# All loads on one queue in order of need, a batch's stack in two halves, maxima in groups of four heads

## The chip, the cores and the metric

The kernel runs on 1 core of one Trainium2 chip. The metric is the device time of one execution in microseconds. The time before is the median of 3 runs.

## What is computed

The reference is a chain of four layers on x of shape 2 x 256 x 128, with a context of 2 x 512 x 128. Layer by layer, cut to what matters here:

```python
x = x + xattn0(layernorm(x), ctx, ctx, mask, Wq, Wk, Wv, Wo, bo)   # 16 heads of 8, masked softmax
x = x + ffn0(layernorm(x), W_router, b_router, W1, b1, W2, b2)     # 8 experts, top 2, 128 -> 512 -> 128
x = x + xattn1(layernorm(x), ctx, cos, sin, ..., Wq, Wkv, Wo, bo)  # 16 heads of 64, ctx normed, rope on k, clip
x = x + ffn1(layernorm(x), weight, bias)                           # ternary weights, inputs rounded to 8 bit
```

In the first attention `scores = q @ k.T / sqrt(8)`, masked, and softmax over the 512 context tokens. Everything is float32. The second attention works on a layer-normed context; its k and v come from `ctx @ Wkv`.

## The kernel before

One program, five engines, each with an instruction stream of its own; the streams meet at semaphores. The order of the work in the middle is a list `order`, written out by hand, which TensorE, VectorE, ScalarE and GpSimd all walk, each doing its part of every item. SyncE only issues DMAs.

**Start.** SyncE loads x, l0w (four 128 x 128 weights), the transposed context `ctxT` in two halves and the context by tokens `ctx_tok` (L317). ScalarE's queue loads the mask twice, lncol, wv1 (the second attention's value weights), rows of ones, and then eight small arrays (L476). VectorE norms x to y (L598 to L609), with GpSimd's power -0.5 in between (L403). TensorE makes k of batch 0, transposes y, makes k of batch 1, q and v. ScalarE copies y transposed (L500), q (L502) and v (L506).

**Stacks.** The scores of the first attention are computed in bfloat16, with k and q each split in three bfloat16 parts, so that their products add up to float32's precision. VectorE splits batch 0 (L633 to L644), GpSimd batch 1 (L426 to L434). For a head, the 8 rows of every part have to stand under each other: `Ks` and `Qs` hold 72 rows of parts, 3 of the mask and 3 of the maxima for each of 16 heads. This layout is made through DRAM: SyncE stores the k parts (L333, three stores of 128 KB, 1 KB rows) to `k_scr` and the q parts (L340, 512 B rows) to `q_scr`, and reads them back into 24 partitions at a time: three reads of 384 KB for k (L343, 16 KB rows) and three of 192 KB for q (L347, 8 KB rows). A whole batch's stack is 1.73 MB. SyncE does batch 0 and then batch 1, in order: stores, mask rows, q store, k reads, q reads. All of it is in one queue.

**Maxima.** Softmax needs the maximum of each row of scores. An item `("mx", q, i)` is a matmul of 128 queries against 512 tokens for one head and VectorE's reduction of it to `nmax` (L661); there are 64, in 4 groups of 16 (8 heads, 2 query tiles). After a group `("mt", q)` transposes its maxima (L916), VectorE and GpSimd split them in three (L670, L671, L444, L445), and SyncE writes them as three rows of `Qs` (L355, 4 KB each), which the scores `("st", u)` of these heads wait for.

**Order of the middle.** Four values (`values(n)`, a matmul of 128 x 512 for the second attention's v) come ahead of it (`EARLY`). Then each of the other twelve values follows two maxima, and two more maxima come. Then 32 units u (batch and head): scores in bfloat16 (four matmuls), one more maximum, the product with v of an earlier unit (`pv`, float32), one more maximum; ScalarE takes the exponential of each unit (L539). The output projection, norm and router of batch 0 are put between units 20 to 29. Then come 16 expert steps (`hid`, `yy`), the second attention, and the last layer. The weights w1, w2, wk1, cosT and sinT are loaded on ScalarE's queue at units 1, 6, 12 and 16 to 19 (L476).

**The context's norm.** VectorE takes the statistics of `ctx_tok` after the q parts (L598), GpSimd the power, VectorE the shift (L650), ScalarE applies them (L511), TensorE transposes, ScalarE writes `ctxT` (L517), and the values follow.

The waits that matter here, in TensorE's part:

```python
if u % 8 == 0:
    pe.wait_ge(max_rows[u // 8], 16 * NPART)
...
if q % 2 == 0 and i == 0:
    ...
    pe.wait_ge(stack[b], 16 * 2 * NPART)
```

## Time and profile before

| what | us |
|---|---|
| median of 3 runs | 285.23 |
| lowest, highest | 282.26, 286.27 |
| the profiled execution | 283.63 |
| its span | 281.9 |
| mean granted TensorE clock | 0.954 of 2.4 GHz |

The span is the time from the first to the last instruction of the profiled execution; its whole time is 1.7 us longer. Shares of the span that the engines are busy: PE 87%, VectorE (DVE) 62%, ScalarE (ACT) 42%, GpSimd (POOL) 16%. PE is TensorE's matmuls, PEld its weight loads, SPq and ACTq are DMA issues on SyncE's and ScalarE's queue. A busy PE is not a PE at its peak: its matmuls overlap, and their ends are modelled. L661 is line 661 of the kernel. A window's columns are: its bounds and length, each engine's busy us with the number of instructions, the granted clock as a fraction, the mean busy share of the 16 DMA engines, and GB/s.

### The profile page before, as it was taken

Reading aid. Unit: us, or ns where it says so; the run is one execution under the profiler, and the core shown is the slowest. Engines: PE = TensorE matmul, PEld = TensorE weight load, DVE = VectorE, ACT = ScalarE, POOL = GpSimd, SP = SyncE. Lnnn points to the kernel's source line nnn. Section 1 sums busy time; section 2 is a strip of 40 time slices with the busy share of each in tenths; the row PEclk is TensorE's granted clock in tenths of the full one; section 3 lists DMA queues with packets and bytes.
Section 4 is the critical chain, followed back from the end, with each engine's and each line's share of the span. In section 5 each row is a group of like instructions: output and inputs, shape, how many; then the busy total and the mean of one; then the engine's idle time right before and its main releaser. Section 6 shows DMA issues by size and latency. Waiting matters only on the chain.

```text
span 281.9 us, 5069 instructions
## 1 busy us (share of the span) xinstructions
PE 244.6 (87%) x2004; PEld 157.2 (56%) x2004; DVE 175.4 (62%) x383; ACT 117.0 (42%) x180; POOL 45.1 (16%) x65
## 2 busy tenths in 40 slices
PE   0632979999999989999999999999979999999941
PEld 0232333343344548888897787886646668666630
DVE  0761049998884341556566962087986975899543
ACT  0226324376667965342424234546336350625000
POOL 2419100000000100051333633001200000100010
PEclk9995579999999999999999999999999999999985
DMA  4958446148721200006005063500000000000001
GB/s 137 239 140 118 113 137 138 45 154 279 203 73 48 76 2 0 2 0 149 3 21 131 0 149 74 136 16 3 0 2 2 0 2 2 0 2 3 2 1 38
DMA packets 13501, 18.63 MB, mean 66 GB/s; under 512 B 2188, under 2 KB 8196, under 8 KB 13188
## 3 DMA queue, kind: packets, MB, share of 16 engines
q1 hardware_dynamic: 9230, 11.95, 18.1%
q10 hardware_dynamic: 4246, 6.34, 7.5%
q8 instruction: 16, 0.26, 0.4%
q14 instruction: 9, 0.07, 0.1%
HBM read 12.45 MB, written 1.45 MB: 49 GB/s over the span
## 4 chain that ended last, share of the span: by engine, by line
PE 63%; issue 13%; DMA 10%; DVE 9%; ACT 2%; POOL 1%; SPq 1%; POOLq 0%; DVEq 0%; ACTq 0%
PE b L848 38%; PE st L848 22%; DVE nmax L661 6%; DMA reg_q<-q_scr 5%; DMA x<-in_x 2%; DMA m_scr<-mpart 2%; DMA q_scr<-reg_z 2%; PE b L947 1%; ACT reg_p L580 1%; ACT reg_p L539 1%; POOL rstd L403 1%; PE b L852 1%; SPq L347 0%; DVE st L598 0%; DVE y L609 0%
## 5 line engine op out<-in xcount | busy, mean ns | idle before, releaser
L661 DVE TENSOR_REDUCE nmax<-b 128x1 f32<-128x512 f32 x64 | 41.3, 685 | 21.0 <-PE b L848 20.9
L848 PE MATMUL b<-reg_p,v 128*32 128x256 f32 (+1 forms) x768 | 50.3, 382 | 1.1 <-ACT reg_z L545 1.1
L580 ACT ACTIVATE reg_p<-st 128x1024 f32<-128x1024 f32 x32 | 31.0, 1022 | 44.4 <-PE st L848 44.4
L557 ACT ACTIVATE reg_z<-st,b 128x256 f32<-128x256 f32 x56 | 24.5, 473 | 32.8 <-PE st L848 32.8
L539 ACT ACTIVATE reg_p<-st 128x1024 f32<-128x1024 f32 x32 | 31.9, 1022 | 9.6 <-PE st L848 6.7
L848 PEld LDWEIGHTS b<-w,reg_z 128*128 128x128 f32 x256 | 30.9, 192 | 4.9 <-issue 4.5
L848 PE MATMUL st<-v,reg_k 64*128 64x256 f32 x256 | 32.0, 389 | 0.3 <-ACT reg_p L580 0.2
L848 PEld LDWEIGHTS b<-reg_p,v 128*32 128x32 f32 (+1 forms) x768 | 19.9, 103 | 22.0 <-issue 9.8
L848 PE MATMUL b<-w,reg_z 128*128 128x128 f32 x256 | 31.5, 276 | 0.0
L794 DVE TENSOR_SCALAR reg_p<-reg_p 128x1024 f32<-128x1024 f32 x32 | 22.5, 703 | 11.3 <-ACT reg_p L580 11.3
L403 POOL TENSOR_TENSOR rstd<-ve,mhalf 128x2 f32<-128x2 f32 (+2 forms) x10 | 8.7, 871 | 123.0 <-DVE ve L603 123.0
L848 PEld LDWEIGHTS st<-v,reg_k 64*128 64x128 f32 x256 | 23.7, 186 | 7.9 <-issue 3.8
L848 PE MATMUL b<-reg_k,reg_q 75*128 75x512 bf16 x64 | 23.6, 396 | 4.1 <-DMA reg_q<-q_scr 2.3
L848 PE MATMUL st<-yT,w 128*128 128x256 f32 x112 | 26.8, 382 | 0.0
L848 PEld LDWEIGHTS st<-yT,w 128*128 128x128 f32 x112 | 20.2, 190 | 2.8 <-issue 0.4
L801 DVE TENSOR_TENSOR w<-reg_p 128x512 f32<-128x512 f32 x30 | 20.8, 692 | 1.0
L848 PE MATMUL st<-reg_p,ctxT 128*128 128x512 f32 x32 | 19.7, 722 | 1.0 <-ACT ctxT L517 1.0
L760 DVE SCALAR_TENSOR_TENSOR x<-b,wgt,x 128x128 f32<-128x128 f32 x32 | 9.6, 342 | 16.0 <-PE b L848 16.0
L848 PEld LDWEIGHTS b<-reg_k,reg_q 75*128 75x128 bf16 x64 | 6.2, 98 | 23.7 <-DVE nmax L661 20.3
L848 PE MATMUL st<-reg_q,reg_k 78*128 78x256 bf16 x128 | 19.2, 273 | 0.1
L496 ACT ACTIVATE v<-st 128x512 f32<-128x512 f32 x16 | 9.6, 597 | 18.7 <-PE st L848 18.7
L806 DVE RECIPROCAL rs<-b 128x256 f32<-128x256 f32 x8 | 14.0, 1752 | 3.7 <-PE b L848 3.7
(158 smaller groups left out, 264.5 us busy)
## 6 DMA issues: line engine op xcount, KB each, us to landing
reg_k<-k_scr SPq DMA_DIRECT2D x6, 384.0 KB
w<-in_w ACTq DMA_DIRECT2D x1, 2048.0 KB, 9.2
reg_k<-reg_p SPq DMA_DIRECT2D x16, 128.0 KB, 2.3
reg_k<-reg_q SPq DMA_DIRECT2D x16, 128.0 KB, 2.3
reg_q<-q_scr SPq DMA_DIRECT2D x6, 192.0 KB
k_scr<-reg_z SPq DMA_DIRECT2D x6, 128.0 KB
ctxT<-in_ctxT SPq DMA_DIRECT2D x2, 256.0 KB, 7.5
reg_p<-in_wv ACTq DMA_DIRECT2D x1, 512.0 KB, 8.5
```

The costliest lines, as they stand in the source:

```text
L403: nc.gpsimd.tensor_tensor(rstd[:, first:first + tiles], ve[:, first:first + tiles], mhalf[:, :].broadcast_to([P, tiles]), ALU.pow).then_in ...
L496: nc.scalar.activation(v1[:, n // 2, 512 * (n % 2):512 * (n % 2) + 512], bank[n % 4], ACT.Copy).then_inc(v1_sb, 1)
L539: nc.scalar.activation(prob[:, u % RING, :], st2[u % 2][:, :], ACT.Exp).then_inc(st_exp, 1)
L557: nc.scalar.activation(hT[:, n % 2, f, :], hidden(n, f), ACT.Relu, bias=b1[:, n % E, f:f + 1]).then_inc(h_sb, 1)
L580: nc.scalar.activation(prob[:, u % RING1, :], st2[u % 2][:, :], ACT.Exp, scale=DK1 ** -0.5).then_inc(st_exp, 1)
L661: nc.vector.tensor_reduce(nmax[:, q, i:i + 1], bank[4 + mx % 2], AX.X, ALU.max, negate=True).then_inc(mx_done, 1)
L760: last = nc.vector.scalar_tensor_tensor(out=x[:, b * QT + t, :], in0=bank[4 + n % 2][:, t * D:(t + 1) * D], scalar=wgt[:, b * QT + t, e:e ...
L794: nc.vector.tensor_scalar(prob[:, u % RING1, :], prob[:, u % RING1, :], math.exp(-CLIP), math.exp(CLIP), ALU.max, ALU.min).then_inc(clippe ...
L801: nc.vector.tensor_tensor(hsum[:, u % RING1, :], prob[:, u % RING1, 0:2 * S], prob[:, u % RING1, 2 * S:4 * S], ALU.add).then_inc(summed, 1)
L806: nc.vector.reciprocal(rs1[:, g % 2, :], bank[7][:, 0:S]).then_inc(rs_sb, 1)
L848: return nc.tensor.matmul(o, l, r, start=start, stop=stop)
L852: last = nc.tensor.transpose(dst[:, t * P:(t + 1) * P], src[:, first + t, :], ident[:, :])
```

## The change

- Every load at the start is issued on SyncE's queue: x, context by tokens, l0w, first half of the transposed context, the two masks, its second half, wv1, and the small arrays, seven of which are packed on the host in one array `small`, and b2. x, ctx, l0w, w1, w2 and wo1 are laid out on the host so that each partition's row is one piece. cosT and sinT are one array, loaded once.
- On VectorE the context's statistics stand before the norm's application to x and before k and q parts; the shift stands between k and q parts. ScalarE norms the context before it copies v, and signals each half. It also runs one exponential on a constant early (`warm`).
- TensorE makes q before k of batch 1.
- Batch 0's stack is read in two halves of eight heads (rows of 8 KB and 4 KB), each with a semaphore of its own. Batch 1's stack is read as before. Its four stores are issued on ScalarE's queue, the three of k ahead of ScalarE's copies of the values and the one of q after the second.
- Six values come ahead of the middle instead of four, ten after pairs of maxima, and no extra maxima before the first scores. Units 0 to 7 have three maxima each, later ones two.
- Maxima are grouped by four heads: 8 groups of 8, so 8 transposes, splits and 3-row writes, and scores wait for a group every 4 units. The rows are 2 KB each.
- w1, w2, wk1 and the rotation tables are loaded at units 6, 11, 16 and 18.

```diff
@@ -216,27 +218,26 @@
...
         order = []
-        maxima = [("mx", q, i) for q in range(2 * B) for i in range(H)]
+        maxima = [("mx", q, i) for q in range(QG) for i in range(4 * QT)]
...
                     order.append(("mt", order[-1][1] - 1))
-            if order[-1][0] == "st" and ("mt", 2 * B - 1) not in order:
-                order.append(("mt", 2 * B - 1))
+            if order[-1][0] == "st" and ("mt", QG - 1) not in order:
+                order.append(("mt", QG - 1))
...
             order.append(("v1", n))
-        next_maxima(3 * H // 2 + 2 - 2 * (2 * CT - EARLY))
...
             order.append(("st", u))
-            next_maxima(1)
+            next_maxima(2 if u < 8 else 1)
@@ -316,44 +317,55 @@
...
 
-            load(x[:, :, :], a["x"].rearrange("t p d -> p t d"), in_x)
-            load(l0w[:, :, :], a["l0w"].rearrange("n p d -> p n d"), in_w0)
+            load(x[:, :, :], a["x"], in_x)
+            load(ctx_tok[:, :, :], a["ctx"], in_ctx)
+            load(l0w[:, :, :], a["l0w"], in_w0)
             load(ctxT[:, 0:S2], a["ctxT"][:, 0:S2], in_ctxT0)
+            load(maskb[:, :], a["mask"].broadcast_to([P, C]), in_maskb)
+            load(mask16[:, :], a["mask"].rearrange("a (p n) -> (a p) n", p=16), in_mask)
             load(ctxT[:, S2:2 * S2], a["ctxT"][:, S2:2 * S2], in_ctxT1)
-            load(ctx_tok[:, :, :], a["ctx"].rearrange("t p d -> p t d"), in_ctx)
+            load(wv1, a["wv1"], in_wv)
+            load(small[:, :], a["small"], in_small)
+            load(b2[:, :], a["b2"], in_small)
...
             sp.dma_start(m_scr.rearrange("j (p n) -> p j n", p=16), mpart[:, :, :]).then_inc(scr_m, 16)
-            for b in range(B):
-                kp = kparts if b == 0 else kparts1
-                qp = qparts if b == 0 else qparts1
-                done = parts if b == 0 else parts1
-                for j in range(NPART):
-                    sp.wait_ge(done, j + 1)
-                    sp.dma_start(k_scr[b, :, j], kp[:, j, :]).then_inc(scr_k[b], 16)
-                if b == 0:
-                    sp.wait_ge(scr_m, 16)
-                    for c in range(B):
-                        sp.dma_start(Ks[MASK_ROW:MASK_ROW + NPART, c, :, :],
-                                     m_scr[:, None, c * S2:(c + 1) * S2].broadcast_to([NPART, H, S2])).then_inc(mask_rows, 16)
-                sp.wait_ge(done, NPART + 1)
-                sp.dma_start(q_scr[b].rearrange("i p t -> p i t"), qp).then_inc(scr_q[b], 16)
-                sp.wait_ge(scr_k[b], 16 * NPART)
+            for j in range(NPART):
+                sp.wait_ge(parts, j + 1)
+                sp.dma_start(k_scr[0, :, j], kparts[:, j, :]).then_inc(scr_k[0], 16)
+            sp.wait_ge(scr_m, 16)
+            for c in range(B):
+                sp.dma_start(Ks[MASK_ROW:MASK_ROW + NPART, c, :, :],
+                             m_scr[:, None, c * S2:(c + 1) * S2].broadcast_to([NPART, H, S2])).then_inc(mask_rows, 16)
+            sp.wait_ge(parts, NPART + 1)
+            sp.dma_start(q_scr[0].rearrange("i p t -> p i t"), qparts).then_inc(scr_q[0], 16)
+            sp.wait_ge(scr_k[0], 16 * NPART)
+            for n in range(2):
+                heads = slice(n * H // 2, (n + 1) * H // 2)
                 for i in range(NPART):
-                    sp.dma_start(Ks[i * STACK:(i + 1) * STACK, b, :, :].rearrange("p h t -> p (h t)"),
-                                 k_scr[b].rearrange("d j h t -> (d j) (h t)")).then_inc(stack[b], 16)
-                sp.wait_ge(scr_q[b], 16)
+                    sp.dma_start(Ks[i * STACK:(i + 1) * STACK, 0, heads, :].rearrange("p h t -> p (h t)"),
+                                 k_scr[0, :, :, heads, :].rearrange("d j h t -> (d j) (h t)")).then_inc(stack[0][n], 16)
+                sp.wait_ge(scr_q[0], 16)
                 for i in range(NPART):
-                    sp.dma_start(Qs[i * STACK:(i + 1) * STACK, b, :, :].rearrange("p h t -> p (h t)"),
-                                 q_scr[b, i].rearrange("(d h) t -> d (h t)", h=H)[:, None, :]
-                                 .broadcast_to([DK0, NPART, H * S])).then_inc(stack[b], 16)
-
-            for q in range(2 * B):
-                b, h0 = q // 2, 8 * (q % 2)
+                    sp.dma_start(Qs[i * STACK:(i + 1) * STACK, 0, heads, :].rearrange("p h t -> p (h t)"),
+                                 q_scr[0, i].rearrange("(d h) t -> d h t", h=H)[:, heads, :].rearrange("d h t -> d (h t)")[:, None, :]
+                                 .broadcast_to([DK0, NPART, H // 2 * S])).then_inc(stack[0][n], 16)
+            sp.wait_ge(scr_k[1], 16 * NPART)
+            for i in range(NPART):
+                sp.dma_start(Ks[i * STACK:(i + 1) * STACK, 1, :, :].rearrange("p h t -> p (h t)"),
+                             k_scr[1].rearrange("d j h t -> (d j) (h t)")).then_inc(stack[1][0], 16)
+            sp.wait_ge(scr_q[1], 16)
+            for i in range(NPART):
+                sp.dma_start(Qs[i * STACK:(i + 1) * STACK, 1, :, :].rearrange("p h t -> p (h t)"),
+                             q_scr[1, i].rearrange("(d h) t -> d (h t)", h=H)[:, None, :]
+                             .broadcast_to([DK0, NPART, H * S])).then_inc(stack[1][0], 16)
+
+            for q in range(QG):
+                b, h0 = q // G, 4 * (q % G)
...
                 for j in range(NPART):
-                    sp.dma_start(Qs[MAX_ROW + j:MAX_ROW + j + 1, b, h0:h0 + 8, :].rearrange("j h (t n) -> j (h t) n", t=QT),
-                                 maxpart[:, q, j, :]).then_inc(max_rows[q], 16)
+                    sp.dma_start(Qs[MAX_ROW + j:MAX_ROW + j + 1, b, h0:h0 + 4, :].rearrange("j h (t n) -> j (h t) n", t=QT),
+                                 maxpart[:, q % G, j, :]).then_inc(max_rows[q], 16)
@@ -475,21 +487,13 @@
...
 
-            load(maskb[:, :], a["mask"].broadcast_to([P, C]), in_maskb)
-            load(mask16[:, :], a["mask"].rearrange("a (p n) -> (a p) n", p=16), in_mask)
-            load(lncol[:, :], a["lncol"], in_cols)
-            load(wv1, a["wv1"], in_wv)
...
                           onesb[:, None, :].broadcast_to([NPART, B * H // 2, S2])).then_inc(in_ones, 16)
-            for dst, name in ((bias0, "bias0"), (brow, "brow"), (bias1, "bias1"), (bias2, "bias2")):
-                load(dst[:, :], a[name].broadcast_to([P, dst.shape[1]]), in_small)
-            load(wr[:, :], a["wr"], in_small)
-            load(b1[:, :, :], a["b1"], in_small)
-            load(b2[:, :], a["b2"], in_small)
-            load(wf[:, :], a["wf"], in_small)
+            act.wait_ge(consts, 1)
+            nc.scalar.activation(warm[:, :], mhalf[:, :], ACT.Exp)
@@ -501,23 +505,30 @@
...
 
+            act.wait_ge(ctx_shift, 1)
+            for c in range(CT):
+                last = nc.scalar.activation(ctx_tok[:, c, :], ctx_tok[:, c, :], ACT.Identity, scale=rstd[:, c:c + 1],
+                                            bias=shift[:, c:c + 1])
+                if c % 4 == 3:
+                    last.then_inc(ctx_normed, 1)
...
                                      ACT.Copy).then_inc(v0_sb, 1)
-            act.wait_ge(ctx_shift, 1)
-            for c in range(CT):
-                last = nc.scalar.activation(ctx_tok[:, c, :], ctx_tok[:, c, :], ACT.Identity, scale=rstd[:, c:c + 1],
-                                            bias=shift[:, c:c + 1])
-            last.then_inc(ctx_normed, 1)
-            act.wait_ge(in_cols, 16)
+            act.wait_ge(in_small, 16 * 2)
...
                                      scale=lncol[:, 2:3], bias=lncol[:, 3:4]).then_inc(ctxn, 1)
+            for j in range(NPART):
+                act.wait_ge(parts1, j + 1)
+                act.dma_start(k_scr[1, :, j], kparts1[:, j, :]).then_inc(scr_k[1], 16)
...
                 values(n)
+                if n == 1:
+                    act.wait_ge(parts1, NPART + 1)
+                    act.dma_start(q_scr[1].rearrange("i p t -> p i t"), qparts1).then_inc(scr_q[1], 16)
@@ -627,8 +637,16 @@
...
             norm_stats(x, 0, TT)
-
+            dve.wait_ge(in_ctx, 16)
+            for c in range(CT):
+                last = nc.vector.bn_stats(st[:, c, :], ctx_tok[:, c, :])
+            link(last)
             norm_apply(y, x, 0, TT)
+            for c in range(CT):
+                last = nc.vector.bn_aggr(mv[:, c, :], st[:, c, :])
+            link(last)
+            nc.vector.tensor_scalar_add(ve[:, 0:CT], mv[:, 0:CT, 1], EPS).then_inc(stats, 1)
+            norms[0] += 1
@@ -637,18 +655,16 @@
...
             part(nc.vector.tensor_tensor(kparts[:, 2, :], res, kparts[:, 1, :], ALU.subtract))
+            dve.wait_ge(pow_done, 2)
+            nc.vector.scalar_tensor_tensor(out=shift[:, :], in0=mv[:, 0:CT, 0], scalar=-1.0, in1=rstd[:, 0:CT],
+                                           op0=ALU.mult, op1=ALU.mult).then_inc(ctx_shift, 1)
...
             part(nc.vector.tensor_tensor(qparts[:, 2, :], res2, qparts[:, 1, :], ALU.subtract))
-            dve.wait_ge(in_ctx, 16)
-            norm_stats(ctx_tok, 0, CT, at=0)
...
             nc.vector.tensor_tensor(kf[:, S2:2 * S2], bank[5], maskb[:, S2:2 * S2], ALU.mult).then_inc(kf_sb, 1)
-            dve.wait_ge(pow_done, 2)
-            nc.vector.scalar_tensor_tensor(out=shift[:, :], in0=mv[:, 0:CT, 0], scalar=-1.0, in1=rstd[:, 0:CT],
-                                           op0=ALU.mult, op1=ALU.mult).then_inc(ctx_shift, 1)
@@ -853,8 +871,11 @@
...
             def values(n):
+                pe.wait_ge(ctxn, 2 if n >= CT else 1)
...
                     pe.wait_ge(v1_sb, n - 3)
+                elif n == 1:
+                    pe.wait_ge(ctxn, 2)
@@ -869,22 +890,21 @@
...
             transposes(y, 0, TT, bank[7]).then_inc(tr, 1)
+            pe.wait_ge(yT_sb, 1)
+            mm(bank[6], l0w[:, 0, :], yT[:, :]).then_inc(q0_ps, 1)
...
             mm(bank[5], l0w[:, 1, :], ctxT[:, S2:2 * S2]).then_inc(k0_ps, 1)
-            pe.wait_ge(yT_sb, 1)
-            mm(bank[6], l0w[:, 0, :], yT[:, :]).then_inc(q0_ps, 1)
...
 
-            pe.wait_ge(ctx_normed, 1)
             for i in range(2):
+                pe.wait_ge(ctx_normed, i + 1)
...
             pe.wait_ge(v0_sb, 2)
-            pe.wait_ge(ctxn, 2)
@@ -899,27 +919,29 @@
...
                     _, q, i = item
-                    b, h, t = q // 2, 8 * (q % 2) + i // 2, i % 2
-                    if q % 2 == 0 and i == 0:
-                        if b == 0:
-                            pe.wait_ge(kf_sb, 2)
-                            pe.wait_ge(mask_rows, 16 * B)
-                            pe.wait_ge(in_ones, 16 * 2)
-                        pe.wait_ge(stack[b], 16 * 2 * NPART)
+                    b, h, t = q // G, 4 * (q % G) + i // QT, i % QT
+                    if q == 0 and i == 0:
+                        pe.wait_ge(kf_sb, 2)
+                        pe.wait_ge(mask_rows, 16 * B)
+                        pe.wait_ge(in_ones, 16 * 2)
+                    if i == 0 and q < G:
+                        pe.wait_ge(stack[0][q // 2], 16 * 2 * NPART)
+                    elif i == 0:
+                        pe.wait_ge(stack[1][0], 16 * 2 * NPART)
...
                     q = item[1]
-                    pe.wait_ge(mx_done, (q + 1) * H)
-                    nc.tensor.transpose(bank[7][0:H, 0:P], nmax[:, q, :],
+                    pe.wait_ge(mx_done, (q + 1) * 4 * QT)
+                    nc.tensor.transpose(bank[7][0:4 * QT, 0:P], nmax[:, q, :],
...
                     b, h = u // H, u % H
-                    if u % 8 == 0:
-                        pe.wait_ge(max_rows[u // 8], 16 * NPART)
+                    if u % 4 == 0:
+                        pe.wait_ge(max_rows[u // 4], 16 * NPART)
```

## Rows read from the trace of the kernel before

**Rows 1.** Busy time by stretch: us; PE, PEld, DVE, ACT, POOL (count); clock, DMA share, GB/s.

```profile
37.16:56.76 19.60, 18.95 (x52) 7.04 (x52) 16.27 (x27) 7.17 (x12) 0.70 (x2) 0.91 0.41 97
56.76:86.60 29.84, 28.30 (x232) 11.95 (x232) 26.31 (x44) 20.05 (x23) 1.39 (x4) 1.00 0.56 173
86.60:104.19 17.59, 16.23 (x181) 8.39 (x182) 7.02 (x32) 14.45 (x19) 1.41 (x3) 1.00 0.12 41
104.19:271.00 166.81, 163.08 (x1488) 120.58 (x1488) 110.14 (x228) 64.56 (x108) 26.75 (x25) 1.00 0.13 30
```

**Rows 2.** Chain of waits up to the first maximum: start, us, what.

```profile
0.80 6.10 DMA x<-in_x
...
17.80 4.79 DMA q_scr<-reg_z
...
24.07 12.95 DMA reg_q<-q_scr
37.16 0.84 PE b L848 x2
```

**Rows 3.** Timeline, first 37 us: start, us, engine, line, what [idle before].

```profile
12.05 1.28 ACT L500 ACT_TABLE_LOAD   x1 [12.05 <-issue]
...
13.29 0.69 DVE L639 TENSOR_TENSOR reg_z<-reg_z 128x512 bf16<-128x512 f32 x1
...
16.97 0.43 DVE L644 TENSOR_TENSOR reg_z<-reg_z 128x256 bf16<-128x256 f32 x1
...
17.43 1.64 DVE L598 BATCH_NORM_STATS2 st<-ctx_tok 128x6 f32<-128x128 f32 x8
...
21.80 0.56 DVE L650 SCALAR_TENSOR_TENSOR shift<-mv,rstd 128x8 f32<-128x8 f32 x1 [1.25 <-POOL rstd L403]
...
24.32 1.15 POOL L429 TENSOR_TENSOR reg_z<-xb,reg_z 128x512 bf16<-128x512 f32 x1
...
28.55 6.35 PE L848 MATMUL st<-reg_p,ctxT 128*128 128x512 f32 x8 [0.96 <-ACT ctxT L517]
```

**Rows 4.** Timeline of SyncE's DMA queue: when each was issued.

```profile
24.75 1.85 SPq L333 DMA_DIRECT2D k_scr<-reg_z  x3
...
38.98 1.11 SPq L343 DMA_DIRECT2D reg_k<-k_scr  x3
...
53.05 1.85 SPq L355 DMA_DIRECT2D reg_q<-maxpart  x3
```

**Rows 5.** DMA issues of the whole run: KB each, us from issue to landing.

```profile
wk<-in_wk ACTq DMA_DIRECT2D x1, 512.0 KB, 3.2
...
q_scr<-reg_y SPq DMA_DIRECT2D x1, 192.0 KB, 11.6
reg_q<-maxpart SPq DMA_DIRECT2D x12, 4.0 KB, 2.2
```

**Rows 6.** Windows around the two stacks' loads, columns as in the first group.

```profile
18.57:37.02 18.45, 8.31 (x16) 4.02 (x16) 2.95 (x15) 7.13 (x14) 8.54 (x10) 0.63 0.68 135
37.02:38.98 1.96, 1.82 (x4) 0.94 (x5) 1.29 (x2) 0.00 (x0) 0.00 (x0) 0.59 0.22 72
38.98:51.70 12.72, 12.45 (x35) 4.45 (x33) 10.32 (x17) 4.89 (x9) 0.00 (x0) 0.93 0.59 139
```

**Rows 7.** Timeline, 50 to 90 us, around the maxima and scores.

```profile
51.60 0.27 DVE L670 CAST maxpart<-b 16x128 bf16<-16x128 f32 x1
...
54.94 7.64 DVE L661 TENSOR_REDUCE nmax<-b 128x1 f32<-128x512 f32 x12 [0.37 <-PE b L848]
...
62.87 0.60 PE L848 MATMUL st<-reg_q,reg_k 78*128 78x256 bf16 x4
```

**Rows 8.** Timeline, 81 to 105 us: scores of unit 19, two exponentials, the first expert.

```profile
85.71 0.60 PE L848 MATMUL st<-reg_q,reg_k 78*128 78x256 bf16 x4
...
88.58 2.17 ACT L539 ACTIVATE reg_p<-st 128x1024 f32<-128x1024 f32 x2
...
104.19 1.05 PE L848 MATMUL b<-reg_p,v 128*9 128x256 f32 x16 [1.13 <-ACT reg_z L545]
```

96 lines of the change are left out of this document (49 added, 47 removed).

## The prediction

> **What bounds the kernel now.** First the busy time by stretch [rows 1]. From 104.19 us on TensorE is busy 163.08 of 166.81 us at full clock, and the diff leaves that part as it is apart from loads that are due long before their use. So the change is worth what it does to the moment at which the first expert starts, 104.19 [rows 8]. Ahead of that are three stages: from the first maximum at 37.16 to the first scores at 56.76 VectorE reduces for 16.27 of 19.60 us; from there to 86.60 VectorE (26.31 of 29.84) and TensorE (28.30) are both nearly full; then TensorE and ScalarE finish the units. Before 37.16 nothing is full. The chain of waits says what ends that stretch [rows 2]: x lands at 6.90, the last store of q parts takes 4.79, and the last read of batch 0's stack lands 12.95 us after its issue, at 37.02. The transfers are the bound there. The window shows 135 GB/s, at a DMA share of 0.68 [rows 6]: not a full set of engines.
>
> The rows of SyncE's queue show something else [rows 4, 5]: batch 1's three k stores were issued from 24.75, yet the wait behind them ended only at 38.98, and the q store landed after 11.6 us; both came in just after batch 0's stack. That queue works in order of issue. The reader should keep this: it decides the forecast.
>
> **The change, part by part.**
>
> *Start.* x goes out alone at the head with whole rows. The nearest row is a 512 KB load with long rows in a quiet queue, 3.2 us [rows 5]; x is half of it, so at best it lands at 0.8 + 3.2 = 4.0, at worst as now. I take 4.3, 2.6 earlier. ScalarE's table load of 1.28 us, which now stands between the transposes and the copy of yT [rows 3], moves to a time at which ScalarE waits for nothing but data: 1.28 off the q path. Against that, the context statistics (1.64 [rows 3], and half as much again for the aggregation, 2.4) are put on VectorE ahead of the k parts and the q parts. The k parts gain 2.6 - 2.4, and an estimated 0.6, as VectorE fills its wait for rstd with them: they end at 13.2 instead of 13.29 + 0.69 = 13.98. The q parts end now at 17.40 [rows 3]. After the change VectorE comes to them at 13.2 plus 0.56 for the shift, and needs 1.55 for four instructions of 0.3 to 0.4: 15.3, 2.1 earlier. If x and the context land late, both gains are gone.
>
> *Stack of batch 0.* Now its reads run from 18.57 to 37.02, 18.45 us [rows 6]. After the change k reads are issued 0.8 earlier, at 17.8, and q reads when the q store has landed: 15.6 + 4.79 = 20.4. The first maximum needs half of the stack, 0.86 MB of 1.73. At the rate of now that is 9.2 us, 27.0; at the faster rate of batch 1's stack (1.73 MB in 12.72 us) 6.2 us, and no sooner than 24.7, when half of the q rows follow their issue. I take 26.5, as most of the wait is the slow rate's. The first maximum moves from 37.16 to 26.5, 10.7 earlier.
>
> *Six values ahead of it.* Four took 6.35 us at the lower clock level [rows 3], so six take 9.5 there and 4.8 at full clock. The shift is ready at 13.8 instead of 22.36, and values began 6.2 after it: they start near 20 and end between 25 and 30. In the second case maxima start at 30. ScalarE now also issues batch 1's four stores; each waits for GpSimd's parts, the last k part now being done at 25.47 and then some 6 earlier, at 19.5. Behind these waits stand the values' copies, and TensorE's fifth value waits for the first copy. That is inside the same 25 to 30.
>
> *Second half and batch 1's stack.* The second half is needed eight value steps later. A step of one value and two maxima costs 19.60 / 13 = 1.5 us [rows 1], so at 38.5. It lands about 17.8 + 18.45 = 36.2: hidden, with 2 us to spare. Batch 1's stack no longer waits for its stores behind batch 0: the gap from 37.02 to 38.98 goes. It follows at once: 36.2 + 12.72 less some 1.5 us of first latency, which a filled queue hides: 47.4. With batch 1's rate for both stacks it is 43; with the stores (0.58 MB) taking their share of the engines, 49.
>
> *Groups of four heads.* Eight transposes instead of four. Each costs VectorE 0.27 and as much again for the subtraction [rows 7]. The first scores need only the first group: after ten steps and twenty maxima, 26.5 + 15 = 41.5, if nothing else holds them.
>
> *But the max rows.* They leave on SyncE's queue too, each a 4 KB write, 2.2 us from issue to landing when the queue is empty [rows 5]. Now they are issued at 53.05, after batch 1's stack (the window at 139 GB/s ends at 51.70) [rows 6]. After the change they are issued at about 35, behind six reads of which the last lands near 47. By [rows 4] they wait for these. So the first scores start at 47.3, not 41.5; everything behind them on TensorE, maxima too, stands for 6 us, and VectorE with it. The 10.7 us are won at the first maximum and mostly given back here.
>
> *From first scores to first expert.* Now 104.19 - 56.76 = 47.43: five units in 6.11, fourteen from 62.87 to 85.71 at 1.63 each [rows 7, 8], thirteen in 18.48. After the change twenty maxima are done instead of twenty-six. Units 0 to 7 carry 24 at 7.64 / 12 = 0.64 each [rows 7], 15.3, plus three groups of 0.55: 16.9, set by VectorE. Units 8 to 17 take 16.3, plus 0.7 for the more frequent transposes. The last fourteen take 18.48 plus one unit; two exponentials take 2.17 [rows 8], so 1.1: 19.6. TensorE has idled and comes back at the lower clock, as in the row of 37.02 to 38.98 (0.59) [rows 6]; VectorE sets the pace there, so I charge 0.5. Sum 16.9 + 17.0 + 19.6 + 0.5 = 54.0.
>
> *Later loads.* w1, w2, keys and rotation tables are issued some units later and in fewer pieces. They are needed from 104 on, and a 512 KB load takes 3.2 us; nothing. The small ones before, eight issues on ScalarE, are off the path. If w2 came later than the first expert, it would cost the difference.
>
> **Sum.** First expert at 47.3 + 54.0 = 101.3, 2.9 earlier than 104.19. The profiled execution took 283.63 (span 281.9): 280.7. It lies 1.6 below the median of the three runs, 285.23; from the median the same gain gives 282.3. I forecast 281.3.
>
> **A rule against it.** The store row shows that batch 1's stores waited behind batch 0's stack on the one queue [rows 4]; moved to ScalarE's queue I let them pass it. The Trainium skill ("DMA: Bandwidth & Descriptors", section "Issuing engines are not separate DMA queues") says that transfers of all issuing engines run on the same 16 engines and interleave, so that a second issuing engine saves little but its own issue time. By that rule the gap would stay, and the result is the fourth case below; no row of before has stores and stack on different queues, so none decides it.
>
> **The rivals.**
> 1. *The forecast's mechanism*: max rows in line behind batch 1's stack, first scores at 45.5 to 49.5. 279 to 284.5. Chance 0.48.
> 2. *A fast stack.* Both stacks at the second's rate: for it, the first stack's slow stretch falls together with GpSimd's and ScalarE's work [rows 6], which ends earlier; against it, GpSimd splits in just this stretch still. First scores at 43.4, first expert 97.4: 276.8. Chance 0.15.
> 3. *The rows pass.* So small a write, on an engine that is free, passes the reads. Against it stand both stores of [rows 4, 5]. First scores at 41.5, gain 8.7: 274.9. Chance 0.12.
> 4. *The stores still come last* (the other side). Rows of 1 KB alternate with stack rows of 8 KB and land only when batch 0's stack is in, at 38.2; batch 1's stack then takes 12.72 as now: 50.9, first scores 51.3, first expert 105.3, 1.1 later: 284.7. It decides from the point where first scores pass 50.2, that is, stores landing after 37.1. Chance 0.18.
> 5. *Slower by more*: reads in half rows are slower per byte. At 10% of 30 us of reads it is 3 us more, 286 to 288 with the fourth case. Chance 0.07.
>
> **How the numbers follow.** About 2% (5.7 us) is what a measurement of this kernel can tell from no change. Faster than 279.5: all of cases 2 and 3 and a sixth of case 1, 0.35. Slower than 291: only case 5 at its worst, 0.04. The rest, 0.61, is within 2%. The range of 8 in 10 leaves a tenth on either side: 274.5 at the fast end, just below case 3, and 286.5 at the slow end, by case 4 from the median (285.23 + 1.1). Case 1's own range is 279 to 284.5.
>
> **What the changed profile would show.** First maximum at 25 to 30 and the yT copy without a table load before it; a wait of TensorE's first scores for the write of max rows, some 6 us, with VectorE idle; the second group of stack reads starting before 38; first expert near 101. The forecast is wrong if the max rows land within 3 us of their issue at 35 (case 3), if batch 1's stores land after 37 (case 4), or if from first scores to first expert it isn't about 54 us.

## The result and the profile after

| | before | after |
|---|---|---|
| median (lowest to highest), us | 285.75 (282.26 to 286.30) | 306.87 (305.67 to 309.78) |
| span of the profiled execution | 281.9 | 303.9 |
| mean granted TensorE clock | 0.954 | 0.874 |
| first maximum | 37.16 | 30.17 |
| first scores | 56.76 | 53.01 |
| first expert | 104.19 | 126.50 |

Four executions each on one chip: ratio 1.082, 95% interval 1.0765 to 1.0875. The change makes the kernel slower, where no change was forecast. Ratios, here and below, leave out the executions that took over 1.5% longer than the fastest of their kernel; among them are seven of the 76 executions of the kernel before that stand beside these kernels (296.20 to 305.64 us, at mean clocks of 0.87 to 0.91, where its others have 0.95 to 0.97).

The windows of the kernel after, by stage; the columns are those of [rows 1] (length, PE, PEld, DVE, ACT, POOL, granted clock, DMA share, GB/s):

```profile
18.79:30.17 11.38, 8.83 (x16) 3.88 (x17) 0.12 (x1) 6.45 (x12) 6.52 (x9) 0.70 0.73 183
30.17:44.90 14.73, 14.18 (x42) 5.27 (x42) 13.32 (x24) 5.40 (x10) 1.39 (x4) 1.00 0.71 108
44.90:53.01 8.11, 0.00 (x0) 0.00 (x1) 0.21 (x1) 0.57 (x1) 0.00 (x0) 0.80 0.32 86
53.01:60.00 6.99, 6.27 (x21) 2.63 (x21) 4.42 (x8) 2.41 (x3) 0.10 (x1) 0.50 0.00 0
60.00:80.00 20.00, 19.14 (x82) 6.62 (x81) 13.67 (x24) 7.18 (x8) 1.99 (x6) 0.50 0.29 106
80.00:100.00 20.00, 20.00 (x106) 5.93 (x104) 10.70 (x19) 7.54 (x8) 1.39 (x4) 0.50 0.29 107
100.00:110.00 10.00, 9.98 (x58) 3.35 (x55) 3.38 (x7) 4.48 (x5) 0.69 (x2) 0.50 0.38 107
110.00:126.50 16.50, 15.37 (x168) 8.35 (x166) 6.47 (x29) 13.45 (x17) 0.71 (x1) 0.97 0.10 33
...
126.50:293.00 166.50, 163.08 (x1488) 120.57 (x1488) 109.88 (x226) 64.57 (x108) 26.74 (x25) 1.00 0.13 30
```

The last row answers to the last of [rows 1]: TensorE is busy 163.08 us in both kernels. So the 22.0 us by which the spans differ are all there at the first expert (126.50 - 104.19 = 22.3). TensorE idles from 44.90 to 53.01. Its clock falls to 0.50 (1.2 GHz) inside this wait, between 49 and 50, and is 0.50 in every row from 53.01 to 110, 57 us in which TensorE is busy 55.39 us. It is the bound there, at half speed, where before the clock was 1.00 [rows 1].

The timeline of the kernel after (start, us, engine, line, what, idle before and who ended it):

```profile
3.54 0.87 DVE L608 BATCH_NORM_STATS2 st<-x 128x6 f32<-128x128 f32 x4 [3.54 <-DMA x<-in_x]
...
13.64 0.69 DVE L657 TENSOR_TENSOR reg_z<-reg_z 128x512 bf16<-128x512 f32 x1
15.97 0.17 DVE L659 SCALAR_TENSOR_TENSOR shift<-mv,rstd 128x8 f32<-128x8 f32 x1 [1.64 <-POOL rstd L415]
...
17.17 0.43 DVE L665 TENSOR_TENSOR reg_z<-reg_z 128x256 bf16<-128x256 f32 x1
...
22.46 2.10 SPq L350 DMA_DIRECT2D reg_q<-q_scr  x3
...
30.17 0.59 PE L866 MATMUL b<-reg_k,reg_q 75*128 75x512 bf16 x2 [1.33 <-DMA reg_q<-q_scr]
...
53.01 1.03 PE L866 MATMUL st<-reg_q,reg_k 78*128 78x256 bf16 x4 [8.18 <-DMA reg_q<-maxpart]
...
90.62 1.06 PE L866 MATMUL st<-reg_q,reg_k 78*128 78x256 bf16 x4
...
93.41 1.06 PE L866 MATMUL st<-reg_q,reg_k 78*128 78x256 bf16 x4
```

The four score matmuls of a unit take 1.03 to 1.06 us, where [rows 7] has 0.60, and a unit takes 2.79 us (90.62 to 93.41) where before it took 1.63. What held the first scores is in the chain of waits:

```profile
24.93 21.18 DMA q_scr<-reg_y
46.11 0.02 issue
46.12 0.66 SPq L359
...
48.19 0.67 SPq L367
...
49.59 3.37 DMA reg_q<-maxpart
52.96 0.05 issue
53.01 1.03 PE st L866 x4
```

and in the DMA issues (KB, us from issue to landing), which answer to [rows 5]:

```profile
x<-in_x SPq DMA_DIRECT2D x1, 256.0 KB, 2.7
...
q_scr<-reg_y ACTq DMA_DIRECT2D x1, 192.0 KB, 21.2
...
mask<-in_mask SPq DMA_DIRECT2D x1, 1.0 KB, 7.8
```

Batch 1's query store, now on ScalarE's queue, took 21.2 us, where it took 11.6 behind the stack on SyncE's. SyncE's instructions stood still until it had landed, at 46.12, and behind that wait stand not only batch 1's query reads but the maximum rows, whose data had been ready since 38.9 for the first group.

### The profile page after: what moved, and what is told of

Same layout as the page of the kernel before. It is cut to its first block, busy times and chain, and to the rows that moved or that the text cites. A ratio compares the mean times of both kernels' runs of the same rounds, so it can differ in the third digit from the quotient of the medians.

```text
span 303.9 us, 5133 instructions
## 1 busy us (share of the span) xinstructions
PE 266.2 (88%) x2008; PEld 162.2 (53%) x2008; DVE 177.3 (58%) x391; ACT 117.3 (39%) x180; POOL 48.8 (16%) x73
## 4 chain that ended last, share of the span: by engine, by line
PE 66%; issue 12%; DMA 11%; DVE 3%; ACT 3%; POOL 2%; SPq 2%; POOLq 0%; DVEq 0%; ACTq 0%
PE b L866 40%; PE st L866 24%; DMA q_scr<-reg_y 7%; DMA mask<-in_mask 3%; DVE nmax L677 1%; DMA reg_q<-maxpart 1%; ACT ctx_tok L510 1%; POOL rstd L415 1%; SPq L318 1%; PE b L969 1%; ACT reg_p L590 1%; SPq L359 1%; ACT reg_p L549 1%; PE b L870 0%; SPq L367 0%
## 5 line engine op out<-in xcount | busy, mean ns | idle before, releaser
L677 DVE TENSOR_REDUCE nmax<-b 128x1 f32<-128x512 f32 x64 | 42.2, 686 | 41.4 <-PE b L866 41.0
L866 PE MATMUL b<-reg_p,v 128*32 128x256 f32 (+1 forms) x768 | 57.0, 421 | 1.1 <-ACT reg_z L555 1.1
L567 ACT ACTIVATE reg_z<-st,small 128x256 f32<-128x256 f32 x56 | 24.5, 473 | 32.8 <-PE st L866 32.8
L866 PE MATMUL st<-reg_q,reg_k 78*128 78x256 bf16 x128 | 28.6, 369 | 8.2 <-DMA reg_q<-maxpart 8.2
L866 PE MATMUL b<-reg_k,reg_q 75*128 75x512 bf16 x64 | 32.2, 549 | 3.4 <-DVE nmax L677 1.6
L812 DVE TENSOR_SCALAR reg_p<-reg_p 128x1024 f32<-128x1024 f32 x32 | 22.5, 703 | 11.3 <-ACT reg_p L590 11.3
L866 PEld LDWEIGHTS st<-reg_q,reg_k 78*128 78x128 bf16 x128 | 15.3, 127 | 23.1 <-issue 9.6
L866 PEld LDWEIGHTS b<-reg_k,reg_q 75*128 75x128 bf16 x64 | 7.5, 119 | 27.4 <-DVE nmax L677 21.8
L866 PE MATMUL st<-reg_p,ctxT 128*128 128x512 f32 x32 | 17.9, 674 | 0.6 <-ACT ctxT L522 0.6
```

The source lines that it names most:

```text
L567: nc.scalar.activation(hT[:, n % 2, f, :], hidden(n, f), ACT.Relu, bias=b1[:, n % E, f:f + 1]).then_inc(h_sb, 1)
L677: nc.vector.tensor_reduce(nmax[:, q, i:i + 1], bank[4 + mx % 2], AX.X, ALU.max, negate=True).then_inc(mx_done, 1)
L812: nc.vector.tensor_scalar(prob[:, u % RING1, :], prob[:, u % RING1, :], math.exp(-CLIP), math.exp(CLIP), ALU.max, ALU.min).then_inc(clippe ...
L866: return nc.tensor.matmul(o, l, r, start=start, stop=stop)
```

## The experiments

Two things could bring the clock down: the idle stretch of 8.11 us ahead of the first scores, and the three maxima in each of the first eight units, for which VectorE sets the pace while TensorE is partly idle. The first theory says that either is enough, its rivals that only one of them does it, or some other part of the change. All times are medians with the range; the ratio is that of the result above, so it need not be that of the medians, and where a kernel's executions lie far apart none is given. Low clock is where windows of the profiled execution show 0.50 behind 44 us, to within 1 us.

| kernel | us | ratio to before | first scores | low clock | first expert |
|---|---|---|---|---|---|
| after | 306.87 (305.67 to 309.78) | 1.082 | 53.01 | 50 to 111 | 126.50 |
| e1_busy_wait | 307.48 (306.95 to 307.83) | 1.081 | 55.37 | 59 to 113 | 128.01 |
| e3_rows_first | 298.61 (298.17 to 302.12) | 1.053 | 47.74 | 52 to 103 | 118.99 |
| e4_q_on_sync | 307.25 (304.88 to 308.69) | 1.079 | 54.37 | 53 to 111 | 127.25 |
| e5_rows_on_scalar | 288.19, 288.78, 305.45, 307.32 | | 50.72 | 53 to 74 | 109.13 |
| e6_before_three | 302.83 (301.01 to 305.03) | 1.071 | 59.24 | 68 to 102, 105 to 109 | 125.90 |
| e12_before_wait | 306.30 (303.65 to 312.53) | 1.065 | 65.47 | 63 to 118 | 133.09 |
| e7_two_maxima | 290.86 (288.96 to 293.73) | 1.027 | 53.06 | 53 to 84 | 112.51 |
| e8_two_rows_scalar | 294.64 (290.33 to 297.15) | 1.031 | 53.36 | 50 to 95 | 117.26 |
| e9_filler | 294.76 (280.93 to 297.35) | | 52.84 | 52 to 76 | 115.48 |
| e10_two_busy | 283.07 (280.99 to 284.35) | 0.993 | 56.76 | 50 to 54 | 104.39 |
| e14_rows_first_two | 286.54 (283.64 to 290.53) | 1.004 | 50.49 | 52 to 69 | 104.44 |
| e15_rows_between | 284.90 (284.25 to 289.32) | 1.005 | 50.33 | 52 to 69 | 105.02 |
| e11_old_order | 289.44 (280.53 to 299.87) | | 53.65 | none | 101.28 |
| e13_old_order_filler | 285.25 (281.24 to 291.59) | 0.998 | 55.40 | 55 to 58 | 105.66 |
| e17_fill_maxima | 282.17 (278.53 to 285.28) | | 52.71 | none | 100.66 |
| e16_fill_both | 280.98 (278.09 to 282.65) | 0.992 | 51.48 | none | 100.57 |

### Is it the wait, or the three maxima?

**The wait filled.** Ten f32 matmuls run where TensorE would wait:

```diff
+                    if u == 0:
+                        pe.wait_ge(v1_sb, 2 * CT)
+                        for _ in range(10):
+                            mm(bank[2], ctxT[:, 0:P], ctxT[:, 0:512])
                     if u % 4 == 0:
                         pe.wait_ge(max_rows[u // 4], 16 * NPART)
-                    if u == 0:
-                        pe.wait_ge(v1_sb, 2 * CT)
```

> The changed kernel with ten more float32 matmuls of 128 x 512 on TensorE (0.86 us each at full clock, result unused) between the last value and the wait for the first group's max rows, the 8.2 us in which TensorE stood. Nothing else is changed, the late rows (53.0) least of all. Clock theory: the granted clock fell in that wait and stayed at half up to 110 us, which cost about 19 us; with the filler it stays at 1.0, the first scores start at 53 to 54, the first expert 54 us later (the forecast's sum for this stage) at 107 to 108, and the time is 286 to 288. Order theory: three maxima to a unit and twice as many groups are slow by themselves, the clock only follows; then the time stays at 303 or more. Both partly: in between, and the clock row of 56 to 110 says which share.

Windows of this kernel:

```profile
44.00:53.00 9.00, 8.31 (x21) 3.53 (x20) 2.24 (x5) 1.19 (x2) 0.70 (x2) 1.00 0.42 84
53.00:57.00 4.00, 3.43 (x13) 1.37 (x12) 0.77 (x2) 0.99 (x1) 0.00 (x0) 1.00 0.03 10
57.00:60.00 3.00, 2.59 (x12) 1.33 (x13) 2.91 (x5) 1.06 (x2) 0.00 (x0) 0.79 0.00 0
60.00:80.00 20.00, 19.14 (x81) 6.34 (x80) 13.40 (x26) 7.02 (x8) 2.10 (x6) 0.50 0.29 106
```

The clock holds through the stretch that was idle, and falls 3 us into the units, with VectorE busy 2.91 of 3.00 us. The time is that of after. The wait is not needed for the loss, though in the kernel after the clock fell inside it, before any unit had begun.

**Three maxima alone, in the kernel before.** Its order of work is changed in one place:

```diff
-            next_maxima(1)
+            next_maxima(2 if u < 8 else 1)
```

> The kernel before, with one change of its order: units 0 to 7 carry three maxima each instead of two (26 ahead of the first scores as before; groups, loads and queues as before). Pace theory: with three maxima VectorE sets the pace (3 x 0.64 = 1.9 us a unit) and TensorE, which has 4 short bfloat16 matmuls of scores and 3 of maxima to do, is idle about half of a unit; that alone drops the granted clock to half, and it stays there until the maxima are over: 298 to 305. Wait theory: only a long idle stretch of TensorE drops it; here there is none, so the time is 282 to 287, as before.

```profile
56.00:60.00 4.00, 3.62 (x15) 1.39 (x13) 3.42 (x6) 1.31 (x3) 0.00 (x0) 1.00 0.04 7
60.00:64.00 4.00, 2.90 (x16) 1.22 (x15) 3.90 (x7) 2.38 (x3) 0.00 (x0) 1.00 0.30 30
64.00:68.00 4.00, 2.98 (x15) 1.13 (x14) 3.93 (x8) 1.91 (x3) 0.70 (x2) 0.95 0.95 359
68.00:72.00 4.00, 3.84 (x17) 1.08 (x17) 3.32 (x5) 1.74 (x2) 0.00 (x0) 0.50 0.37 139
72.00:90.00 18.00, 18.00 (x92) 5.60 (x88) 9.86 (x16) 6.55 (x8) 0.70 (x2) 0.50 0.42 119
```

This edit costs the kernel before 7.1% (interval 1.062 to 1.081), nearly all that the whole change does. Its four executions took 301.01 to 305.03; beside them the kernel before took 280.95 to 286.22 in five and 296.87 and 303.71 in two. The rows from 60 to 68 show it in the units: VectorE busy 3.90 and 3.93 of 4.00, TensorE 2.90 and 2.98. Then the clock falls, and TensorE becomes the bound: 18.00 of 18.00 us busy.

**A wait alone, in the kernel before.** GpSimd runs 64 short memsets behind its first maximum group, and the first scores wait for the last:

```diff
+                    if item[1] == 0:
+                        for _ in range(63):
+                            link(nc.gpsimd.memset(hold[:, :], 0.0))
+                        nc.gpsimd.memset(hold[:, :], 0.0).then_inc(held, 1)
...
+                        pe.wait_ge(held, 1)
```

> The kernel before with one addition: GpSimd runs 64 small memsets one after the other behind its first maximum group (53.0), and the first scores wait for the last of them; two maxima in a unit as before. This puts an idle stretch of 3 to 9 us in front of the first scores and changes nothing else. If an idle stretch alone is enough to bring the clock down for the units behind it, the granted clock falls to 0.50 within the first units, the stage behind the first scores takes 60 us or more where before has 47.4, and the time is 298 or more. If only the pace of three maxima does it, the stage keeps its 47.4, and the time rises by the added wait alone: 287 to 293, with a clock of 1.00 in the units.

```profile
58.00:62.00 4.00, 0.53 (x2) 0.10 (x1) 1.46 (x3) 0.56 (x1) 2.56 (x26) 1.00 0.00 0
62.00:65.47 3.47, 0.00 (x1) 0.03 (x2) 0.00 (x0) 0.00 (x0) 2.17 (x21) 0.64 0.00 0
65.47:68.00 2.53, 2.53 (x11) 1.43 (x11) 1.06 (x2) 1.02 (x1) 0.00 (x0) 0.50 0.03 6
68.00:112.00 44.00, 44.00 (x210) 15.07 (x208) 24.01 (x39) 18.57 (x21) 1.39 (x4) 0.50 0.37 114
```

6.84 us of idle TensorE, with two maxima in a unit, cost 6.5% (1.059 to 1.072). So an idle stretch is enough too. The last row is the surprise: TensorE is busy 44.00 of 44.00 us and stays at 0.50. (This profiled execution took 312.53 us, the longest of the four; the ratio is that of the two at 303.65 and 303.69.)

**Neither, in the kernel after.** 26 maxima ahead and two in a unit, first with the wait as it comes, then with five f32 matmuls in it:

```diff
+        next_maxima(6)
...
-            next_maxima(2 if u < 8 else 1)
+            next_maxima(1)
```

> The changed kernel with the old spread of the maxima: 26 ahead of the first scores and two to a unit; groups of four heads, loads, queues and stores as changed. The max rows still land at 53, TensorE stands from about 49 to 53. Pace theory: after that wait units run at 1.3 to 1.6 us with TensorE nearly full; the clock may dip in the wait but comes back, first expert at about 53 + 48 = 101 plus some us for the dip: 281 to 287. Wait theory: the wait drops the clock and it stays down: 300 to 307.

> The changed kernel with 26 maxima ahead of the first scores and two in each unit of scores, as the kernel before has it, and with five f32 matmuls of 128x128x512 that keep TensorE at work while it would wait for the maximum rows. It computes the same output beside them. Of the two things that can bring the clock down, the three maxima of a unit and the idle stretch, both are gone. If these two are the whole cause, the granted clock stays 1.00 through the units, the stage from the first scores (near 54) to the first expert takes the 47.4 us of before, the first expert starts at 101 to 102, and the time is 280 to 283. If something else of the change brings the clock down (half stacks, the reads of batch 1's stack beside the scores, maxima in groups of four), it falls to 0.50 all the same and the time is 290 or more, as with two maxima and the wait (290.86).

With the wait, 2.74 us of it, 290.86; with it filled, 283.07 (ratio 0.9926, interval 0.989 to 0.997, all ten executions below 284.4). Windows of the second:

```profile
48.00:50.00 2.00, 1.17 (x3) 0.31 (x4) 2.00 (x4) 0.35 (x1) 0.00 (x0) 1.00 0.54 86
...
51.00:52.00 1.00, 1.00 (x4) 0.48 (x3) 0.95 (x3) 0.00 (x0) 0.00 (x0) 0.50 0.62 115
...
53.00:54.00 1.00, 1.00 (x3) 0.43 (x2) 0.00 (x0) 0.00 (x0) 0.26 (x1) 0.60 0.31 73
54.00:55.00 1.00, 1.00 (x3) 0.38 (x2) 0.00 (x0) 0.00 (x0) 0.00 (x0) 1.00 0.09 29
...
58.00:60.00 2.00, 1.66 (x10) 0.60 (x7) 2.00 (x4) 1.51 (x3) 0.00 (x0) 1.00 0.00 0
```

The clock did fall, between 50 and 51, and came back some 3 us later, among the f32 matmuls. The first row shows what stands ahead of the fall: the six added maxima come behind the last value, so that TensorE is busy 1.17 of 2.00 us while VectorE reduces. That is a third place of the same kind. e8_two_rows_scalar, further below, has the same order and repeats it: TensorE is busy 1.21 of 2.00 us from 48 to 50 and the clock falls between 50 and 51, ahead of its wait. In neither had a unit of scores begun or TensorE stood still for long. Half stacks, reads beside the scores and groups of four are all still in this kernel, so none of them costs what the change costs.

### Where the wait comes from

**The rows issued ahead of the wait for the query store**, groups 0 and 1 only:

```diff
+            rows_out(0, 2)
             sp.wait_ge(scr_q[1], 16)
...
-            for q in range(QG):
+            rows_out(2, QG)
```

> The changed kernel, with the max rows of groups 0 and 1 issued on SyncE's queue before it waits for batch 1's q store (landed only at 46.1) and reads the q stack. Sequencer theory: what held the rows was SyncE's own wait for that store; issued at 39 they have only the k reads of batch 1 ahead (data until 48), so they land at 47 to 48.5, first scores near 48, TensorE's idle stretch shrinks from 8.1 to 3 us; if the clock holds, 281 to 283, if it falls all the same, 299 to 301. Queue theory (the forecast's): rows wait for everything queued before them, here only the k reads, same landing; it differs in e4. If the rows pass the reads: landing near 42, first scores at 45.

First scores at 47.74, 5.3 earlier; first expert 7.5 earlier; 298.61. The rows were issued from 40.97 and the first group's landed some 5 us behind the last of its three issues.

**Batch 1's query store on SyncE's queue**, ahead of the second half's reads:

```diff
+                if n == 1:
+                    sp.wait_ge(parts1, NPART + 1)
+                    sp.dma_start(q_scr[1].rearrange("i p t -> p i t"), qparts1).then_inc(scr_q[1], 16)
```

> The changed kernel, with only batch 1's q store back on SyncE's queue, ahead of the reads of batch 0's second half. Sequencer theory: the store lands by 30 instead of 46.1, SyncE issues everything by 34 and the max rows at 39 and 45; if that wait was all, first scores come at 45 and the time is 279 to 283. Queue theory: the rows then stand in the queue behind the whole of batch 1's stack, whose last q rows come at 50 to 52, so the first scores start at 50 to 53, the clock falls as before, and the time is 302 to 307, no gain from the store.

DMA issues, and then the timeline, of this kernel:

```profile
q_scr<-reg_y SPq DMA_DIRECT2D x1, 192.0 KB, 6.8
```

```profile
41.59 7.87 SPq L370 DMA_DIRECT2D reg_q<-maxpart  x6
...
54.37 1.03 PE L866 MATMUL st<-reg_q,reg_k 78*128 78x256 bf16 x4 [6.89 <-DMA reg_q<-maxpart]
```

The store took 6.8 us from SyncE's queue, issued at 24.27, against 21.2 from ScalarE's, issued at 24.93. (Its place is another one too: on SyncE's queue it stands ahead of the second half's reads.) SyncE then came to the rows at 41.59, without a wait for the store, but all of batch 1's reads were in the queue, and the first group's rows landed at 54.3, 11.3 us after the third of them was issued. So the in-order queue of the forecast is there, and it costs as much as the stalled sequencer: 54.37 against 53.01.

**The rows on ScalarE's queue**, after values 12 and 15, then with two maxima, then with a filler matmul in the first eight units:

```diff
+                    if item[1] in (12, 15):
+                        q = 0 if item[1] == 12 else 1
+                        act.wait_ge(mt_parts, q + 1)
+                        for j in range(NPART):
+                            act.dma_start(Qs[MAX_ROW + j:MAX_ROW + j + 1, 0, 4 * q:4 * q + 4, :].rearrange("j h (t n) -> j (h t) n", t=QT),
+                                          maxpart[:, q, j, :]).then_inc(max_rows[q], 16)
...
+                    if u < 8:
+                        mm(st2[u % 2][:, 0:256], ctxT[:, 0:P], ctxT[:, 0:256])
```

> The changed kernel, with the max rows of groups 0 and 1 issued on ScalarE's queue, after its copies of values 12 and 15. Neither SyncE's wait nor its queue is ahead of them; on ScalarE's queue only the last packets of the q store are. If they land within 2 to 6 us as that theory says, first scores start at 45 to 46, TensorE has no long idle stretch, the clock stays at 1.0, and the first expert comes at 99 to 100: 278 to 280. If packets of that queue get one turn per 16 KB packet as the q store did (21.2 us), they land with it near 46 to 50, and the clock decides: 282 with, 300 without.

> e7 with the first two groups' max rows on ScalarE's queue (as in e5). First scores at 50 to 51 with 26 maxima done by 49: next to no idle. Both theories: the clock holds, first expert near 51 + 48 + 1 = 100, 279 to 281. If e5's two kinds of execution (288 and 306) appear here too, neither the three maxima nor the wait is what decides.

> e5 (three maxima to a unit, first rows on ScalarE's queue) with one more float32 matmul of 128 x 256 (0.43 us at full clock, its result overwritten) in each of units 2 to 7. Pace theory: it fills the idle half of a unit, VectorE still sets the pace, so it costs nothing in itself; the clock holds or comes back sooner, and all executions are 283 to 288. If it is not the idle share but the bfloat16 matmuls' own kind that drops the clock: 288 and 306 as in e5, plus 1 to 3.

(The fillers of e9 are in units 0 to 7; its expectation says 2 to 7.) These three settled little. The rows left late, since ScalarE comes to them between its values, and landed about 5 us later; an idle stretch of 2.2 to 4.3 us remained in all. With it, e5 took 288 in two executions and 305 to 307 in two, e9 280.93 in one and 295 to 297 in three, and e8 290 to 297, where 279 to 281 was expected. Fillers behind an idle stretch (e9) did not mend it in three of four. What follows is only that a short idle stretch is near an edge.

### Without the wait, by order alone

Two versions with 26 maxima ahead and the rows in time: e14_rows_first_two joins the edits of e3_rows_first and e7_two_maxima; the second has batch 1's query store on SyncE's queue and the first rows ahead of batch 1's key reads as well:

```diff
+            rows_out(0, 1)
             sp.wait_ge(scr_k[1], 16 * NPART)
...
+            rows_out(1, 2)
             sp.wait_ge(scr_q[1], 16)
```

> The changed kernel with the maximum rows of the first two groups issued by SyncE between the key reads and the query reads of batch 1 (they landed at 47.7 when this was done alone), and with 26 maxima ahead of the first scores and two in a unit. TensorE has maxima until about 51, so the rows have landed when the scores want them and no idle stretch is left. If the idle stretch and the three maxima are the whole cause, the clock stays 1.00 behind 50, first scores start at 51 to 52, the first expert at 98 to 101, and the time is 278 to 282. If the clock falls without either, the time is 288 or more.

> As the run before it, and in addition batch 1's query store stands on SyncE's queue ahead of the second half's reads, and the first group's rows ahead of batch 1's key reads, the second group's between key and query reads. By the in-order queue the first rows land with the second half of batch 0's stack, before 42, and batch 1's reads end before 50. The first scores start at 51 to 52 without a wait. If the idle stretch and the three maxima are the whole cause, 278 to 282 in nearly all executions. If batch 1's reads, now delayed behind a wait for the first group, come too late for the 33rd maximum, TensorE waits there and the clock falls: 288 or more.

Both start the first scores at 50.4 without a wait, and both lose the clock all the same, for 17 us. The windows of the first:

```profile
46.00:48.00 2.00, 1.89 (x7) 0.66 (x5) 1.97 (x5) 1.19 (x2) 0.70 (x2) 1.00 0.01 1
48.00:50.00 2.00, 1.21 (x4) 0.29 (x3) 2.00 (x4) 0.00 (x0) 0.00 (x0) 1.00 0.01 2
...
51.00:52.00 1.00, 0.91 (x6) 0.45 (x5) 0.97 (x4) 0.87 (x1) 0.02 (x1) 0.92 0.43 147
52.00:53.00 1.00, 0.98 (x4) 0.11 (x2) 1.00 (x2) 0.63 (x2) 0.68 (x2) 0.50 0.55 188
```

My expectation missed the row from 48 to 50: maxima with no value between them. EARLY back at 4 spreads them again (with the rows after values 10 and 15 on ScalarE's queue, and the query store on SyncE's), first without and then with fillers in the units:

```diff
-EARLY = 6
+EARLY = 4
...
+        next_maxima(2)
```

> The changed kernel's loads, half stacks and groups of four heads, with the order of work nearer to that of before: EARLY back at 4, two maxima more ahead of the first scores, two maxima in each unit, the query store of batch 1 on SyncE's queue ahead of the second half's reads, and the maximum rows of the first two groups issued from ScalarE's queue after its values 10 and 15. If the gain of the loads is there and only order and wait took it back, the first maximum comes at 30, the first scores near 49 with an idle stretch under 3 us, the first expert at 97 to 100, and the time is 277 to 281, if the clock stays at 1.00. If TensorE's stretch is near its edge whatever the order, the clock falls somewhere between 50 and 80 and the time is 286 to 296.

> The version with the old order (EARLY 4, 26 maxima ahead, two in a unit, rows of the first two groups from ScalarE's queue), and in each of the first eight units of scores one f32 matmul of 128x128x256 whose result is overwritten. Its predecessor without them ran at 280.53 in one execution, with TensorE 3.19 of 4 us busy at 52 to 56 and VectorE 3.95, and at 288 to 300 in five. The fillers take TensorE up to some 0.4 us more per unit, in time in which it waits for VectorE. If the fall comes from TensorE's share of busy time in the first units, nearly all executions now keep the clock and the time is 279 to 283. If it does not, or if the fillers push TensorE past VectorE's pace, the executions stay spread over 283 to 300.

Once, in the profiled execution, e11 kept its clock throughout: 280.53, first expert at 101.28. In five others it took 288 to 300. The first scores came at 53.65, not 49: a wait of 0.38 us was left, and VectorE was the pace from 40 to 60 (3.67 to 3.97 of every 4.00 us). With fillers all twelve stayed below 291.6, at mean clocks of 0.948 to 0.974, but in the profiled one TensorE still waited for the rows from 52 to 54.46, and the clock dipped for 3 to 4 us.

### The stretch of maxima filled, and the units too

On e14_rows_first_two, a short f32 matmul ahead of each of the last maxima, and for the second kernel one in each of the first eight units:

```diff
+                    if 22 <= mx <= 26:
+                        if mx == 22:
+                            pe.wait_ge(v1_sb, 2 * CT)
+                        mm(bank[2][:, 0:256], ctxT[:, 0:P], ctxT[:, 0:256])
...
+                    if u < 8:
+                        mm(st2[u % 2][:, 0:256], ctxT[:, 0:P], ctxT[:, 0:256])
```

> The run with the maximum rows in time, and one f32 matmul of 128x128x256 (result not used) ahead of each of the last maxima before the first scores, where TensorE was busy 1.21 of 2.00 us. If it is this stretch that brings the clock down, it now stays 1.00 behind 50, the first expert starts near 99 and the time is 279 to 282. If the units of scores bring it down by themselves, the clock falls a few us later, as in the run before it, and the time is 284 to 291.

> As the run before it, and one such matmul in each of the first eight units of scores too, where VectorE sets the pace. If TensorE's idle shares are the whole cause, the clock stays at 1.00 from 40 to the end, the first expert starts at 98 to 100 and the time is 278 to 281 in nearly all executions, below both kernels. If the fillers cost more than they save, 282 to 285.

The first: 279.85 and 278.53 at mean clocks of 0.97, 284.48 and 285.28 at 0.94. So with the maxima alone filled, two of four executions still lose some clock. The second: 280.98, twelve executions between 278.09 and 282.65, ratio 0.9918 (0.987 to 0.996), and its slowest execution lies below the median of the kernel before beside it (284.47). Windows of the second:

```profile
46.00:50.00 4.00, 3.53 (x15) 1.96 (x14) 3.31 (x6) 0.83 (x2) 0.70 (x2) 1.00 0.07 11
50.00:54.00 4.00, 3.92 (x24) 2.62 (x23) 3.94 (x8) 1.59 (x2) 0.69 (x2) 1.00 0.45 145
54.00:58.00 4.00, 3.92 (x26) 2.52 (x25) 3.70 (x7) 2.54 (x4) 0.00 (x0) 1.00 0.02 4
58.00:62.00 4.00, 4.00 (x34) 2.08 (x33) 3.40 (x6) 2.35 (x3) 0.70 (x2) 1.00 0.01 2
```

The clock is 1.00 in every window from 38 on. The matmuls whose results nobody reads are nearly free, but not quite: from first scores to first expert the second kernel takes 49.09 us, the first, without fillers in the units, 47.95, and the kernel before 47.43. The first expert comes at 100.57, 3.6 before that of the kernel before, as the first scores come 5.3 earlier. The gain thus lies ahead of the first scores, where the loads, half stacks and early rows act: about 1%. Fillers in the kernel before, the control to this, were not run.

## Why the prediction was wrong

*Start.* x landed at 3.54 (forecast 4.3). The k parts ended at 13.64 + 0.69 = 14.33, not 13.2: the first matmul waited for ctxT until 9.12. The q parts ended at 17.60, not 15.3: VectorE waited 1.64 us for the shift's rstd, until 15.97, as GpSimd stood at the mask, which took 7.8 us to land behind five larger loads, and split it from 11.03 to 13.30 first. I had not asked what moving the mask to the long queue would hold up. Both gains of the start were lost: before had 13.98 and 17.40.

*Stack of batch 0.* The query reads were issued at 22.46, not 20.4, and the first half took 7.7 us behind that, not 6.1: first maximum at 30.17, not 26.5. The mechanism (half the stack is enough) is right, 7.0 us were won, of 10.7 forecast.

*But the max rows.* The step "first scores start at 47.3" failed: 53.01. I let the stores of batch 1 pass on ScalarE's queue. The three k stores did (their wait ended at 29.49), so the fourth rival's condition, stores landing after 37.1, held for the q store alone: it landed at 46.11. The in-order queue, on which the forecast rested, is there behind it (e4_q_on_sync), and gives 54.37 instead of 47.3, as two terms of it were too small: the rows came at 41.6, not 35, since the maxima began at 30.70 there, not 26.5, and went more slowly, and the reads before them ended well past 47: the rate from 30 to 45 was 101 GB/s there and 108 in the kernel after, not the 135 to 139 of [rows 6]. The fourth rival, the other side, put the first scores at 51.3, nearer than the forecast. It had a late store as the reason, but not SyncE's own wait for it, with the rows behind that wait, and its price was 1.1 us in all.

*The rule against it.* The store took 21.2 us on ScalarE's queue, and 6.8 on SyncE's, issued at nearly the same time. The Trainium skill ("DMA: Bandwidth & Descriptors", section "Issuing engines are not separate DMA queues") has transfers of all issuing engines interleave, and a second engine save only the time of issuing. The trace agrees in part: the k stores did land among the reads, so the gap did not stay, but the q store's landing changed threefold, far more than any issue time.

*From first scores to first expert.* Here the time went: 73.5 us (126.50 - 53.01), not 54.0. The failed step is "so I charge 0.5" for the lower clock. I had read the dip of [rows 6] as one that ends by itself, with VectorE as the pace beside it. In the kernel before that dip lasted from 37.4 to 40.8, among maxima with f32 matmuls of the values between them; the units have no such values. Here the clock stayed at 0.50 until 111, 58 us behind the first scores, TensorE became the bound and a unit took 2.79 us. The excess over the forecast is 5.7 us of late first scores and 19.5 us of this; together 25.2, which is 126.5 - 101.3. Of the rivals none had the clock as its mechanism. The three maxima of a unit I priced by VectorE's 0.64 us each, and VectorE kept about that price (686 ns on average in the kernel after, 685 before); what they do to TensorE, which stands partly idle beside them, was not in the sum.

*The range and the chances.* The range ended at 286.5; slower than 291 had a chance of 0.04, all of it from slow reads. The last stage, which the sum leaves as it is (283.63 - 104.19 = 179.4), took 179.2, so the later loads cost nothing, as forecast.

**What stays open.** Shown are three forms of one precursor: an idle TensorE (e12_before_wait), three maxima in a unit (e6_before_three), and maxima with no value between them, behind which the clock fell in e10_two_busy and e8_two_rows_scalar with neither of the others yet there. With all of them filled, e16_fill_both kept its clock in the traced execution, and all twelve had mean clocks of 0.968 to 0.982.

Not shown is why the clock stayed low for 17 to 62 us while the rows have TensorE busy nearly all the time. It came back within about 3 us among the f32 matmuls of e10_two_busy and e13_old_order_filler, but e9_filler, with the same fillers as the latter, stayed low for 24; without any it took 17 us at the soonest. The traces hold one more clue. Twelve profiled executions lost the clock for 17 us or more, and in eleven of them it came back during, or within 2.4 us behind, two f32 products with v that have no scores between them. In the kernel after, where it came back at 111.2 (x8 is one product, x16 are two in a row):

```profile
106.18 1.04 PE L866 MATMUL b<-reg_p,v 128*9 128x256 f32 x8
...
108.12 1.90 PE L866 MATMUL b<-reg_p,v 128*9 128x256 f32 x16
```

Such a pair comes every fourth unit, and three of them (at 75.06, 86.45 and 97.83) passed there without effect. So more f32 work close together is what TensorE did before its clock rose, but that this is the cause is not shown: no run changed the type of the matmuls alone, their 75 to 78 rows, or the gaps that the modelled ends may hide. Nor is it known why the one store starved while its three neighbours passed. Its rows are 512 B, theirs 1 KB, and it was issued later, beside more reads; no run separated these.

## What to carry to other kernels

When a step makes another engine the pace, ask what TensorE does beside it: here a TensorE that idled in part lost half its clock, and then was the bound itself, for far longer than the stretch that caused it. Price each wait and each rebalancing twice, once for its own length and once for the clock behind it, above all where rows of the kernel already show fractions of the clock. And on a queue that carries small urgent rows and long reads, look at both orders: that of the transfers, and that of the issuing engine's own waits.

## What the hardware showed that I had not expected

- TensorE was busy 44.00 of 44.00 us at a granted clock of 0.50 (e12_before_wait), 18.00 of 18.00 (e6_before_three). The Trainium skill ("TensorE: Matmul & The Clock Gate", section "What's actually happening") says that activity releases the throttle; in these rows it did not for tens of us, and in e10_two_busy it did in about 3.
- One line of the order of work, with the same instructions, moved a kernel by 7.1%.
- Matmuls whose result is thrown away made a kernel faster: a ratio of 1.004 (0.993 to 1.014, e14_rows_first_two) became 0.992 (0.987 to 0.996, e16_fill_both).
- A 192 KB store took 21.2 us from ScalarE's queue and 6.8 us from SyncE's, where it stood ahead of the second half's reads.
